# Writing five turns of two hand-ordered loops out per turn of a shorter loop, on four of five engines

## What is computed

```python
# layer 0: hypergraph convolution twice, with relu and a layer norm between (512 -> 1024 -> 512), + x
# layer 1: pairwise weights exp(lrelu(8*tanh((s_i+s_j)/8))) * adj, normalized, applied to x, then @ w
# layer 2: three graph convolutions  adj @ (x @ W) + b, relu between
# layer 3: attention, 8 heads of 64, softmax + 0.33*adj + 0.33*exp(-adj), then @ W_out + b_out
```

## Time and profile before

| | us |
|---|---|
| median of 3 runs | 2844.67 (2843.2 to 2847.39) |
| the profiled execution, its device time | 2846.66 |
| its span, first to last instruction | 2844.9 |
| PE busy | 2659.1 (93% of the span) |
| DVE busy | 1820.5 (64%) |
| ACT busy | 879.0 (31%) |
| POOL busy | 474.9 (17%) |
| mean granted PE clock | 0.978 of full speed |

### The profile page before, as it was taken

The page is one execution under the profiler, slowest core; times in us unless marked ns, Lnnn a source line. Parts: engine busy times, 40 slices in busy tenths (PEclk is TensorE's granted clock), DMA queues, the critical chain, the costliest instruction groups (busy, mean ns, idle before and its releaser), DMA issues.

```text
span 2844.9 us, 73879 instructions
## 1 busy us (share of the span) xinstructions
PE 2659.1 (93%) x30296; PEld 2197.8 (77%) x30296; DVE 1820.5 (64%) x3754; ACT 879.0 (31%) x2397; POOL 474.9 (17%) x749
## 2 busy tenths in 40 slices
PE   3999999999999999299999999999999999999998
PEld 2778778777777778287788788788788778878877
DVE  3778887788878887446545655654654655565565
ACT  2222322222222222233332332333333333233233
POOL 0222222222222222010110111011011011101101
PEclk9999999999999999699999999999999999999999
DMA  5111111111111110201101100100110110110010
GB/s 181 28 38 36 35 35 35 38 36 36 38 36 40 42 35 19 97 6 33 37 8 33 38 13 28 36 25 19 33 31 13 33 38 10 29 38 17 26 32 16
DMA packets 130004, 99.41 MB, mean 35 GB/s; under 512 B 89104, under 2 KB 91152, under 8 KB 129808
## 3 DMA queue, kind: packets, MB, share of 16 engines
q1 hardware_dynamic: 129808, 96.30, 11.4%
HBM read 62.68 MB, written 33.55 MB: 34 GB/s over the span
## 4 chain that ended last, share of the span: by engine, by line
PE 52%; DVE 4%; issue 2%; ACT 1%; SPq 1%; DMA 0%; DVEq 0%; POOLq 0%
PE qs L1109 43%; PE qs L1140 4%; PE qs L1171 1%; PE qs L1178 1%; DVE T2l L1004 1%; PE qs L1150 1%; PE qs L1185 1%; ACT T2h L942 1%; DVE sm L1007 0%; DVE Z L1084 0%; DVE E L1069 0%; DVE E L1073 0%; DMA QK<-in_L_Wqkv 0%; DVE sm L1060 0%; DVE E L1058 0%
## 5 line engine op out<-in xcount | busy, mean ns | idle before, releaser
L1109 PE MATMUL qs<-hi,T2h 128*128 128x512 f32 x1024 | 422.0, 412 | 24.5 <-DVE T2l L1004 24.1
L1109 PE MATMUL qs<-hi,T2l 128*128 128x512 f32 x1024 | 406.9, 397 | 0.0
L1109 PE MATMUL qs<-lo,T2h 128*128 128x512 f32 x1024 | 406.5, 397 | 0.0
L1004 DVE TENSOR_TENSOR T2l<-qs,T2h 128x512 fp32r<-128x512 f32 x320 | 212.9, 687 | 183.1 <-ACT T2h L942 110.9
L864 POOL TENSOR_TENSOR sm<-sm,mhalf 128x1 f32<-128x1 f32 x128 | 86.2, 673 | 1370.6 <-DVE sm L1011 1370.6
L1109 PE MATMUL qs<-T2h,WQh 128*128 128x256 f32 x1024 | 291.2, 284 | 0.0
L1109 PE MATMUL qs<-T2h,WQl 128*128 128x256 f32 x1024 | 288.2, 281 | 0.0
L1109 PE MATMUL qs<-T2l,WQh 128*128 128x256 f32 x1024 | 288.1, 281 | 0.0
L1109 PEld LDWEIGHTS qs<-hi,T2h 128*128 128x128 f32 x1024 | 194.6, 190 | 78.5 <-DVE T2l L1004 34.8
L1109 PEld LDWEIGHTS qs<-hi,T2l 128*128 128x128 f32 x1024 | 194.5, 190 | 46.1
L1109 PEld LDWEIGHTS qs<-lo,T2h 128*128 128x128 f32 x1024 | 195.1, 190 | 39.8
(11 more groups left out here) (175 smaller groups left out, 5319.3 us busy)
## 6 DMA issues: line engine op xcount, KB each, us to landing
X<-in_x SPq DMA_DIRECT2D x64, 256.0 KB, 6.5
x<-R SPq DMA_DIRECT2D x64, 256.0 KB, 2.0
X<-x SPq DMA_DIRECT2D x64, 256.0 KB, 2.9
out<-Z SPq DMA_DIRECT2D x64, 256.0 KB, 3.1
AB<-in_adj SPq DMA_DIRECT2D x512, 8.0 KB, 1.6
A<-in_adj SPq DMA_DIRECT2D x128, 32.0 KB, 2.2
An<-in_adj SPq DMA_DIRECT2D x16, 128.0 KB, 2.3
WB<-in_adj SPq DMA_DIRECT2D x32, 64.0 KB, 7.3
```

Source lines behind the costliest of these rows:

```text
L1004: return dve.tensor_tensor(lo, ps, hi.bitcast(F32), ALU.subtract)
L1109: mm = pe.matmul(out, lhsT, rhs, start=i == 0, stop=i == len(terms) - 1)
```

## The change

`Fori(0, 15)` becomes `Fori(0, 3)` with a body that holds the steps of five turns one after the other. The turn's number is `turn * 5 + part`. The same edit is made on PE, DVE, ACT and POOL, in both parts; SP keeps its loops of 15 turns. Nothing is computed, moved or waited for in another order.

```diff
+UNROLL = 5
...
             steps(START, -1, number)
-            with pe.Fori(0, iters - 1) as it:
-                steps(ORDER, it, pe.to_reg)
+            with pe.Fori(0, (iters - 1) // UNROLL) as turn:
+                for part in range(UNROLL):
+                    steps(ORDER, pe.snap(turn * UNROLL + part), pe.to_reg)
             steps(END, iters - 1, number)
```

More of the change, by code:

```diff
@@ L278, in _ @@
             steps(START, -1, number)
-            with pool.Fori(0, iters - 1) as it:
-                steps(ORDER, it, pool.to_reg)
+            with pool.Fori(0, (iters - 1) // UNROLL) as turn:
+                for part in range(UNROLL):
+                    steps(ORDER, pool.snap(turn * UNROLL + part), pool.to_reg)
             steps(END, iters - 1, number)
@@ L364, in _ @@
             steps(START, -1, number)
-            with act.Fori(0, iters - 1) as it:
-                steps(ORDER, it, act.to_reg)
+            with act.Fori(0, (iters - 1) // UNROLL) as turn:
+                for part in range(UNROLL):
+                    steps(ORDER, act.snap(turn * UNROLL + part), act.to_reg)
             steps(END, iters - 1, number)
@@ L544, in _ @@
             steps(START, -1, number)
-            with dve.Fori(0, iters - 1) as it:
-                steps(ORDER, it, dve.to_reg)
+            with dve.Fori(0, (iters - 1) // UNROLL) as turn:
+                for part in range(UNROLL):
+                    steps(ORDER, dve.snap(turn * UNROLL + part), dve.to_reg)
             steps(END, iters - 1, number)
```

## The result

The changed kernel takes 2819.61 us (median of 4 runs, 2816.09 to 2822.66) beside 2844.13 us for the kernel before on the same chip (4 runs, 2843.2 to 2847.39): ratio 0.9911, 95% interval 0.9894 to 0.9928. That is 24.5 us less; forecast were 32 less.

What follows compares the result with a forecast made beforehand. PE bounds loop 1 (busy 66.97 of 67.70 us); loop 2 idles 5.5 us per turn, mainly at jumps to code not held. Terms -41 - 3 + 10 + 2 = -32 us gave 2812.7 us, range 2800 to 2830.

Steps and rivals of the forecast that it cites:

- second rival: Loop 1, written out, must fetch code all the time: 1 us per turn, 2828 us (0.10); as a loss, 2858 us (0.05).
- "issue" in the middle of turns: Sign of a wrong prediction: PE idle for "issue" spread over its lines in mid-turn; no size given.
- Loop 2, 12 seams, -41: Loop 2's seams that lose their jump: 3.6 us less each, minus 0.2 for DVE's register arithmetic; 41 us less.
- Loop 2, 2 jumps that stay, +2: Loop 2's remaining jumps: PE pays as now, DVE's longer body makes its copy at most 1 us late each; 2 us more.
- Loop 1, 2 jumps, 5.1 us each: Loop 1's remaining jumps: body no longer held, 3.4 us more pause plus 1.7 us from half clock each; 10 us more.
- Loop 1, 12 seams, -3: Loop 1's seams that lose their jump: branch and counter go, 0.24 us each; 3 us less.
- Code streaming slows loop 1: Rival: written-out loop 1 fetches code constantly, 0.13 us a packet, 1 us per turn: 2828 us (0.10); as a loss, 2858 (0.05).
- Loop 1 pays nothing: Rival: loop 1's two jumps find their target or clock stays up, loop 2's seams gain 3.6 us each: 2801 us; chance 0.14.
- The pause isn't the jump's: Rival: loop 2's seam pause comes from register arithmetic or a wait, so it stays; within 3 us of before; chance 0.05.
- Loop 1 pays already: Rival: code held for far less than a turn, so loop 1's jumps already cost loop 2's price; 2772 us; chance 0.01.

Runs made afterwards that it cites:

- u_pe: Against the kernel before, both loops written out five times on PE alone, DVE, ACT and POOL keeping 15 turns: 2820.27 us.
- u_others: Against the kernel before, both loops written out five times on DVE, ACT and POOL, not on PE: 2851.92 us.
- u_loop1: Against the kernel before, only the first part's loop written out five times: 2853.59 us.
- rot2: Kernel before, nothing written out, loop 2's order begun ten steps later so its jump stands behind large products of wo.1: 2866.14 us.
- u_loop2: Against the kernel before, only the second part's loop written out five times, on PE, DVE, ACT and POOL: 2809.11 us.
- rot2_shift48: rot2 plus 48 already fulfilled waits (24 instructions) on PE ahead of part 2, moving loop 2's head just behind a block edge: 2803.7 us.
- before_shift192: Kernel before plus 192 already fulfilled waits (96 instructions) on PE ahead of part 2, nothing else: 2833.73 us.

## Why the prediction was right, and where it was off

The sum was -32 us and the measurement -24.5, inside the range of 2800 to 2830 and, at 2819.61, at the very edge of the 2806 to 2820 of the forecast proper. It is the forecast with some 5 us of the second rival in it, and one of the signs of being wrong that the prediction named, "issue" in the middle of turns, did appear. By its terms:

- **Loop 2, 12 seams, -41.** Right in its mechanism, and in its size by the luck of a balance. A seam without a stall takes 10.92 us, so 3.6 go and not 3.4: the 0.2 us taken off for DVE's register arithmetic was not there. Against that the third seam of each body takes 12.08, 12.46 and 12.17 us, 1.2 to 1.5 more, for a late block. 12 x 3.6 less 3 x 1.3 is 39. Both written-out and kept seams of loop 2 together were forecast at -39 and came to -37.9.
- **Loop 2, 2 jumps that stay, +2.** The mechanism was right: PE waits 1.1 us for DVE's copy at each of the two, and the seams are 1.4 and 0.4 us longer than the mean before, 1.7 in all. u_pe, where DVE's jump is as short as before, has no wait for that copy over 0.7 us.
- **Loop 1, 2 jumps, 5.1 us each.** The pause from L625's product to L565's is 444.68 - 439.86 = 4.82 us, before 1.11, so 3.7 more, and the granted clock was at the lower of its levels for 3.4 us:

```profile
445.70:449.10 3.40, 3.40 (x9) 2.64 (x9) 1.48 (x6) 1.45 (x4) 1.35 (x2) 0.52 0.16 42
```

  Eight products started 445.85 to 449.12, 0.41 us apart, where they start 0.23 apart at full clock, which is 1.4 us. Together 5.1: as forecast, with a pause 0.3 longer and a slow stretch 0.3 cheaper.
- **Loop 1, 12 seams, -3.** This was hardly there, and not for the reason given. From one first product of `y2.2` to the next, the nine turns with neither a jump nor a cut burst take 67.37 to 67.76 us, 67.55 in the mean, where they took 67.61: less than 1 us in all. In u_pe, where only PE's branch goes, such turns take 67.59 to 67.65, as before; in u_others, where PE's branch stays, 67.39 to 67.74. So PE's branch and counter were worth nothing here.
- **What failed: "Code streaming slows loop 1" was left at nothing in the sum.** Loop 1 lost 13.9 us (14.5 from its first product on, since it began 0.6 earlier) and the terms above are 2 x 5.1 - 1 = 9. The other 5 are five cuts like that at 492 us, 4.0 us of idle, 0.6 to 1.3 us from one start to the next and 5.0 in all. A sixth, at 146.92 us, was there before. The rival had the mechanism, and priced it as an even 1 us per turn at 0.13 us per packet. It isn't even: a block that ends under large products costs nothing (most do), and one that ends inside a burst of 64x64 can cost about 1 us. A burst of 64 of these takes 1.07 us from start to start (1491.84 to 1492.91 above), so by my estimate a block of 256 instructions of them lasts 2.1 us; the same number of large products, at 0.23 us each, lasts 29. And the argument against the rival, that one turn of loop 2 takes in 11 packets and waits at the seam alone, was read too quickly: before, "issue" at L1185 and L1171 was such a stall, 3 us in all.
- **"Loop 1 pays nothing"** fell: its branch has two records of about 3.9 us. **"The pause isn't the jump's"** fell: written-out seams have none before their first transposes. **"Loop 1 pays already"** fell in u_loop1, where writing it out only costs. The page behind it, Advanced Engine Details and Errata in the Trainium skill, section on the ISA cache, gives two lines of 256 instructions; the runs disagree, with a body of 1599 instructions and a branch of 208 ns.
- The Trainium skill, Advanced Engine Details and Errata, section on control flow timing, gives about 108 ns for a compare-and-branch. The runs show 208 to 215 ns on PE for a jump to code that is held and medians of 3.3 to 4.2 us for one that isn't, in every kernel.

The Trainium skill, Runtime: NRT & Kernel Launch, section on instruction fetch mechanics, gives most engines 512 instructions. DVE's pause agrees with the direction: in loop 1 it is at none of its jumps with a body of one turn (167 instructions), and at both with five (822). No run here bounds the number from close by.

## What to carry to other kernels

Look at the branch line of a loop before writing it out: on PE here, 0.2 us meant that the body is held and there is nothing to win, 3.5 us that it is fetched anew at each jump. In the second case first place the jump: behind queued long products, with the target just behind a block edge and not just ahead of one. That gave 40 us here, no less than the 35 of writing the same loop out and with hardly more code; the jump moved without the target made the kernel slower. In straight code too, a block edge inside a burst of tiny products can cost about 1 us, so when an unrelated edit moves a kernel by half a per cent, compare where its bursts lie modulo 256 instructions before explaining the edit.

## What the runs showed of the hardware

- PE's stalls in bursts of small products lie at one position of its instruction count modulo 256, which a fetch in blocks of 256 instructions explains. They are 0.4 to 1.9 us of idle each, and 1.8 to 2.3 us behind the jumps of rot2, which land some 12 instructions ahead of an edge.
- A jump to code that isn't held takes 3.3 to 4.5 us in PE's branch record. DVE's own record stays at 60 to 68 ns where its target isn't held, and in loop 1 the 2.6 to 2.9 us stand behind it as "issue" of the next instruction. The branch line alone would have missed it.

```profile
L548 DVEq COMPARE_BRANCH  x3: 60/68/68, 438.9 to 1128.9; - x3
```

- After such a pause the granted clock mostly goes to its lower level, 1.2 GHz, for about 3.4 us, at times for 6.8. It did so behind both jumps of each loop of the changed kernel, and not behind every jump of the kernel before. It stayed at 1.00 behind the cuts of about 1 us in the changed kernel, and fell to 0.57 behind one of 1.89 us in u_loop2 (2077 to 2081 us).
- 24 instructions that do nothing moved this kernel by 2.1% (rot2 to rot2_shift48), and 96 by 0.35% (before to before_shift192).
